# A retrieval-and-projection kernel: loading W in two bursts around tile 0's turn, evacuating before splitting on ScalarE, and giving TensorE two more slots of tile 1

## The reference

```python
retrieved = jnp.mean(item_embeddings[indices], axis=1)         # 512 x 50 indices into a 12500 x 512 table
fused_input = jnp.concatenate([user_rep, retrieved], axis=1)    # 512 x 1024
fused_rep = fused_input @ W_fuse + b_fuse                       # 512 x 512
logits = fused_rep @ W_proj + b_proj                            # 512 x 12500
```

## Time and profile before

| | us |
|---|---|
| median of 3 runs (338.04 to 339.5) | 338.95 |
| the profiled execution | 338.66 |
| its span in the profile | 336.6 |
| TensorE busy (matmuls) | 318.3 (95%) |
| VectorE busy | 184.9 (55%) |
| ScalarE busy | 68.5 (20%) |
| GpSimd busy | 82.3 (24%) |

### The profile page before, as it was taken

The page is one execution under the profiler, slowest core; times in us unless marked ns, Lnnn a source line. Parts: engine busy times, 40 slices in busy tenths (PEclk is TensorE's granted clock), DMA queues, the critical chain, the costliest instruction groups (busy, mean ns, idle before and its releaser), DMA issues.

```text
span 336.6 us, 4239 instructions
## 1 busy us (share of the span) xinstructions
PE 318.3 (95%) x1464; PEld 260.9 (78%) x1464; DVE 184.9 (55%) x317; ACT 68.5 (20%) x102; POOL 82.3 (24%) x84
## 2 busy tenths in 40 slices
PE   4959998599999999999999999999999999999996
PEld 1429876498888898888888888888888888888884
DVE  5899598795678833625454444535354544435222
ACT  2330653530020024022022220222012221020000
POOL 4777778677777100000000000000000000000000
PEclk9996999999999999999999999999999999999999
DMA  7994998989997212786755776568757466442222
GB/s 277 363 396 93 414 383 246 323 270 402 376 338 210 96 62 98 176 333 248 213 162 216 230 243 185 176 249 244 201 161 249 181 213 213 161 166 99 91 91 91
DMA packets 33837, 75.24 MB, mean 224 GB/s; under 512 B 5686, under 2 KB 21830, under 8 KB 33824
## 3 DMA queue, kind: packets, MB, share of 16 engines
q1 hardware_dynamic: 26912, 60.11, 52.2%
q0 software_dynamic: 6336, 13.92, 12.6%
q10 hardware_dynamic: 576, 1.05, 0.8%
HBM read 55.47 MB, written 25.60 MB: 241 GB/s over the span
## 4 chain that ended last, share of the span: by engine, by line
PE 71%; DVE 0%; issue 0%
PE bank L660 69%; PE bank L646 2%; PE bank L636 0%; DVE total L471 0%; DVE out_sb L535 0%
## 5 line engine op out<-in xcount | busy, mean ns | idle before, releaser
L660 PE MATMUL bank<-w_hi,f_hi 128*128 (+1 forms) x400 | 155.8, 390 | 0.0
L660 PE MATMUL bank<-w_lo,f_hi 128*128 (+1 forms) x400 | 155.3, 388 | 0.0
L660 PE MATMUL bank<-w_hi,f_lo 128*128 (+1 forms) x400 | 155.1, 388 | 0.0
L535 DVE TENSOR_TENSOR out_sb<-bank,early 128x500 f32<-128x500 f32 x92 | 62.4, 678 | 128.1 <-PE bank L660 125.5
L660 PEld LDWEIGHTS bank<-w_hi,f_lo 128*128 128x128 f32 x400 | 75.1, 188 | 15.5
L660 PEld LDWEIGHTS bank<-w_hi,f_hi 128*128 128x128 f32 x400 | 75.2, 188 | 15.0
L660 PEld LDWEIGHTS bank<-w_lo,f_hi 128*128 128x128 f32 x400 | 75.2, 188 | 15.0
L327 ACT CAST w_hi<-w_raw 128x1000 fp32r<-128x1000 f32 x46 | 47.1, 1029 | 151.4 <-DMA w_raw<-w_proj 96.4
L267 POOL DMA_INDIRECT ring<-item_embeddings,rows x68 | 71.0, 1045 | 24.8 <-issue 16.6
L507 DVE TENSOR_TENSOR w_lo<-w_raw,w_hi 128x1000 fp32r<-128x1000 f32 (+1 forms) x58 | 55.4, 977 | 2.3 <-ACT w_hi L327 2.3
L471 DVE SCALAR_TENSOR_TENSOR bank<-ring,mask,bank 128x512 f32<-128x512 f32 x56 | 42.1, 752 | 4.5 <-DMA ring<-item_embeddings,rows 1.0
(11 more groups left out here) (60 smaller groups left out, 61.6 us busy)
## 6 DMA issues: line engine op xcount, KB each, us to landing
logits<-out_sb SPq DMA_DIRECT2D x100, 250.0 KB, 2.6
w_raw<-w_proj SPq DMA_DIRECT2D x46, 500.0 KB, 6.9
early<-b_proj SPq DMA_DIRECT2D x25, 250.0 KB, 5.9
early<-w_proj SPq DMA_DIRECT2D x4, 500.0 KB, 6.7
ring<-item_embeddings,rows POOLq DMA_INDIRECT x68, 6.2
early<-user_t ACTq DMA_DIRECT2D x4, 256.0 KB, 4.1
early<-w_fuse SPq DMA_DIRECT2D x4, 256.0 KB, 5.4
wf_ret<-w_fuse SPq DMA_DIRECT2D x1, 1024.0 KB, 19.0
```

What stands on the lines that cost most here:

```text
L535: nc.vector.tensor_tensor(out_sb[:, g % OUT_SLOTS, :], ps[:, 0:CHUNK], bias[:, c % BIAS_SLOTS, 0:CHUNK], ALU.add).then_inc(evacuated, 1)
L660: m = nc.tensor.matmul(ps[:, 0:CHUNK].unsqueeze(1), f[:, t, k, :], w, start=begin, stop=(f is f_lo and k == HK - 1))
```

## The change

Seven edits, all in the order of work:

1. SyncE loads chunks 2 and 3 as soon as slot 12 of tile 0 has landed (before: slot 16), and chunks 4 and 5 when ScalarE has made all of tile 0's `f_hi` (before: right behind chunk 3, where buffers allowed).
2. Chunks 6 and 7 go into the two halves of `early`, no longer into `w_raw`; the eight bias rows are loaded four and four behind the stores of groups 6 and 7, once those halves have been split.
3. ScalarE evacuates groups 0 and 1 before it splits chunks 4 and 5.
4. `PE_LAST` is 4: TensorE sums slots 13 to 16 of tile 1. VectorE's last add for tile 1 is then slot 12, so that the addition of `home` comes last there and writes `total`.
5. The turn of tile t+1 comes behind the whole of group 6, and `fuse` in the middle of group 7.
6. The last eight matmuls of the user half wait one by one for slots 2 to 9 of tile 0.
7. VectorE counts columns (which releases GpSimd's gather of leftovers) behind add 6 of tile 0 (before: add 4), makes `bias_lo` later, and does chunk 1's first low half behind the addition of `home`.

```diff
+BURST_AT = 12
+PACED_AT = 2
-PE_LAST = 2
+PE_LAST = 4
...
         def raw_of(c):
-            return c if c < 4 else c % 2
+            return c % 4 if c < RESIDENT else c % 2
...
             sp.wait_ge(user_fused, 1)
-            sp.wait_ge(slot_landed[place(0, PASSING - 1)], 16 * slot_uses(0, PASSING - 1))
-            for c in range(2, 6):
-                load_chunk(c)
+            sp.wait_ge(slot_landed[place(0, BURST_AT)], 16 * slot_uses(0, BURST_AT))
+            load_chunk(2)
+            load_chunk(3)
+            sp.wait_ge(f_hi_ready, HK)
+            load_chunk(4)
+            load_chunk(5)
             for c in range(RESIDENT):
+                store(0, c)
                 if c < 2:
                     load_chunk(c + 6)
-                store(0, c)
-                if c == RESIDENT - 3:
-                    sp.wait_ge(lo_ready, 8)
-                if c >= RESIDENT - 3:
-                    for b in range(3 * (c - RESIDENT + 3), min(3 * (c - RESIDENT + 4), BIAS_SLOTS)):
+                if c >= RESIDENT - 2:
+                    sp.wait_ge(lo_ready, 2 * c + 2)
+                    for b in range(4 * (c - RESIDENT + 2), 4 * (c - RESIDENT + 3)):
                         load_bias(b)
...
             for c in range(RESIDENT):
-                if c < 2:
-                    split_hi(c + 4)
-                if c == RESIDENT - 2:
+                if c == RESIDENT - 1:
                     mean(1)
-                if c == RESIDENT - 1:
                     fused_hi(1)
                 evacuate_first(c)
                 if c < PE_LAST:
                     keep_last(c)
-                if c in (2, 3):
+                if c < 4:
                     split_hi(c + 4)
...
+                if t and final:
+                    dve.wait_ge(ret_turned, t)
+                nc.vector.tensor_tensor(total[:] if final else total_ps[:], total_ps[:], home[:], ALU.add)\
+                  .then_inc(home_added, 1)
...
-            for i in range(5):
+            for i in range(7):
                 add(0, i)
             count_columns()
-            bias_lo()
-            add(0, 5)
-            add(0, 6)
             split_lo(0, (0,))
             add(0, 7)
             add(0, 8)
+            bias_lo()
...
-            split_lo(1, (0,))
             dve.wait_ge(laps_ready, 1)
             add_home(0)
-            split_lo(1, (1,))
+            split_lo(1)
...
                 for n in range(HK):
+                    if behind is not None:
+                        pe.wait_ge(slot_landed[place(0, behind + n)], 16 * slot_uses(0, behind + n))
...
-                    pe.wait_ge(added, adds_done(1, last_add(1)))
+                    pe.wait_ge(home_added, 2)
...
                     if halfway is not None and k == HK // 2:
-                        turn_sum(halfway)
+                        fuse(halfway)
...
-            user_part(2)
-            user_part(3).then_inc(user_fused, 1)
+            user_part(2, behind=PACED_AT)
+            user_part(3, behind=PACED_AT + HK).then_inc(user_fused, 1)
...
-                    halfway = t + 1 if c == RESIDENT - 2 and t + 1 < TILES else None
-                    project_resident(t, c, halfway)
-                    if halfway is not None:
-                        fuse(halfway)
+                    project_resident(t, c, t + 1 if c == RESIDENT - 1 and t + 1 < TILES else None)
+                    if c == RESIDENT - 2 and t + 1 < TILES:
+                        turn_sum(t + 1)
```

More of the change, by code:

```diff
@@ L153, in raw_of @@
         def raw_of(c):
-            return c if c < 4 else c % 2
+            return c % 4 if c < RESIDENT else c % 2
         def raw_uses(c):
-            return 1 if c < 4 else c // 2
+            return c // 4 + 1 if c < RESIDENT else (c - RESIDENT) // 2 + 3
         def place(t, i):
@@ L192, in load_chunk @@
                     if c >= 4:
-                        sp.wait_ge(lo_ready, 2 * (c - 4 if c < 6 else c - 2) + h + 1)
+                        sp.wait_ge(lo_ready, 2 * (c - 4 if c < RESIDENT + 2 else c - 2) + h + 1)
                     sp.dma_start(raws[raw_of(c)][:, 2 * h:2 * h + 2, :], w_proj[c, :, 2 * h:2 * h + 2, :])\
@@ L455, in count_left, with home_last @@
                 dve.wait_ge(last_landed, 16)
+            def home_last(t):
+                return last_add(t) <= HOME_AFTER
             def add(t, i):
@@ L468, in add @@
                     dve.wait_ge(added, adds_done(t, i - 1))
-                if i == last_add(t):
+                final = i == last_add(t) and not home_last(t)
+                if final:
                     dve.wait_ge(ret_turned, t)
-                nc.vector.scalar_tensor_tensor(total[:] if i == last_add(t) else total_ps[:], here,
+                nc.vector.scalar_tensor_tensor(total[:] if final else total_ps[:], here,
                                                mask[:, t, i + 1:i + 2], total_ps[:], ALU.mult, ALU.add).then_inc(added, 1)
@@ L480, in add_last @@
                     return
-                if t == 1:
-                    dve.wait_ge(home_added, 1)
+                if t == 1 or home_last(t - 1):
+                    dve.wait_ge(home_added, t)
                 else:
@@ L499, in add_home @@
                 dve.wait_ge(home_landed[t], laps * 16)
-                nc.vector.tensor_tensor(total_ps[:] if t else total[:], total_ps[:], home[:], ALU.add).then_inc(home_added, 1)
+                final = t == 0 or home_last(t)
+                if t and final:
+                    dve.wait_ge(ret_turned, t)
+                nc.vector.tensor_tensor(total[:] if final else total_ps[:], total_ps[:], home[:], ALU.add)\
+                  .then_inc(home_added, 1)
             def split_lo(c, halves=(0, 1)):
@@ L608, in _, with user_part @@
         def _(pe):
-            def user_part(k):
+            def user_part(k, behind=None):
                 pe.wait_ge(user_landed[k], 16)
```

## The result

| | before | changed |
|---|---|---|
| median of four runs each, us | 339.23 | 345.61 |
| lowest to highest, us | 338.04 to 339.63 | 344.58 to 347.01 |
| profiled execution, us | 338.66 | 344.58 |
| its span, us | 336.6 | 342.5 |
| mean granted TensorE clock | 0.988 | 0.989 |

The ratio is 1.0197 with a 95% interval of 1.015 to 1.0243: the changed kernel is **slower by about 2%**, where 334.7 us had been forecast in a range of 331.7 to 337.6. The forecast was wrong, and the sign too. Every ratio in this document is taken over those runs of a kernel that lie within 1.5% of its fastest one, which leaves all runs of this pair and of the first batch, but in the later batches only 5 of 25, 12 of 24, 12 of 19 and 12 of 19 runs of the kernel before, and 3 of 10 of x5 in batch 5.

A forecast was written before the change was run, and what follows sets the result against it. TensorE, busy 95% of the span, was taken as the bound. Start -1.9, W -6.1 + 0.3 and slots +1.9 were cut at tile 2's turn to 4.0 us less: 338.66 to 334.7 us, range 331.7 to 337.6.

The forecast's parts named there:

- The start term: Up to tile 0's group 0: pacing, VectorE's order and the early burst together give -1.9 us (-2.3 without contention).
- Rival 2: Start of tile 0: the first burst holds up slot 16, start term +1.1, total 335.3 us; chance 8%.
- W and ScalarE: Tile 0: earlier W and earlier evacuations remove TensorE's stalls, -6.1 us with 0.3 left; ends -6.1 and 0.
- Two more slots: Tile 1's turn: TensorE sums four slots, two more than before, which costs +1.9 us.
- Covered by 1.8 us: Tile 1's turn ends at 62.5, before GpSimd's gathers of tile 2's slots 5 to 8 come up at 64.3.
- Rival 4: Tile 1's turn gates GpSimd's gathers: `home` at 73.9, tile 2 at 103.1, slower at 340.3 us; chance 6%.
- Tile 2's turn: End of tile 1: later place wins 1.36 us, earlier total 2.6; tile 2 starts at 97.4 instead of 101.45.
- the total is ready at 90.4: Tile 2's total, paced by GpSimd's gathers at 1.3 us each, comes 2.6 us earlier than 93.04.
- The three signs of error: Tile 0's last gathers over 5 us, ScalarE getting chunk 7 after 60, GpSimd waiting for TensorE at about 64.

The follow-up runs named there:

- the first batch: Follow-up runs x1 to x4 on the start, beside the kernel before, which took 337.83 us (median of 12 runs).
- x5: x3 with the turns back in the middle of group 6 and fuse between groups 6 and 7; ratios to before 0.9936, 1.0005, 0.9896, 0.9841.
- batch 5: Later follow-up runs of x3, x5 and x12 beside the kernel before, which took 359.63 us there.
- x2: The changed kernel with the column count back behind add 4, burst still at slot 12; 342.92 us, ratio to before 1.0155.
- x3: The changed kernel with the count back behind add 4 and the first burst behind slot 16; 340.69 us, ratio 1.0083; in batch 5 356.6 us, 0.998.
- x1: The changed kernel with the first burst moved back behind slot 16; 343.45 us, ratio to before 1.0181.
- x4: x3 without the pacing of the user half's matmuls; 341.37 us, ratio to before 1.0103.
- x12: x3 with PE_LAST = 2, so two slots fewer on TensorE; 355.01 us, ratio to before 0.9883.
- x6: x3 with chunks 8 and 9 of W loaded later; 353.2, 355.84 and 357.03 us, ratios to before 1.0041, 1.0014, 0.9996.
- x8: The kernel before with chunks 8 and 9 of W loaded later; 358.19 and 357.38 us, ratios to before 1.0073 and 1.0132.

## Why the prediction was wrong, point by point

- **The start term, forecast -1.9, measured +5.4: this is the first step that failed.** Three of its pieces were wrong. Slot 16 was given 1.5 us more by a choice "nearer the first bound" of 2.1 and 6.5 us; slot 13, issued 0.2 us behind the burst, took 7.2, past the far bound. The count of slots behind the burst was wrong: 15 and 16 were named, 13 to 16 it was. Edit 7's later count, which the prediction did not cost, keeps GpSimd waiting 1.83 us and puts slot 13 behind the burst; slot 14 is behind it with the early count too (x2). And the clock, costed as held throughout, fell after the wait (0.66 from 30 to 40 us). Rival 2 named the mechanism but priced it at +1.1 and 8%. With the burst behind slot 16 and the early count (x3) the term is -1.7, where -2.3 had been named without contention: what pacing and VectorE's order bring was put 0.6 us too high.
- The Trainium skill, DMA: Bandwidth & Descriptors (Queues, rings and completion order), which the prediction held against edit 1, says that a DMA engine alternates between its queues packet by packet. Slot 13's 7.2 us against the 2.1 of the earlier trace rows and x2's caught slot 14 agree with it: it should have weighed more than a choice between bounds.
- **W and ScalarE, forecast -6.1 + 0.3: the number came out, under conditions that were not the forecast's.** One stall of 0.65 us is left in tile 0, though chunk 7 came late (ScalarE got its last half at 64.18, where over 60 was named as a sign of error). Chunks 4 to 7 are loaded in step with group 0, so that was 19.7 us behind it, as forecast (57 less 37.2). But from the first burst to group 0 there were 18.3 us, not 10.8. No run had both the early burst and the start at 37: that the stalls would have gone there too is not shown, and x3, with the burst at 31.36, kept 2.2 us of them.
- **Two more slots, +1.9: right** as TensorE's time: 3.57 us from 66.10 to 69.67 for four, against 1.86 for two. **"Covered by 1.8 us" was wrong.** The cover was the distance from the turn's end, put at 62.5, to GpSimd at 64.3. In the changed kernel the gather behind the gate went at 71.5, after 3.4 us of waiting; even in x3, with the good start, it cost 1.5, since the turn of four slots began at 61.53 and ended near 66.1. Rival 4 (6%) had the gate and the place (slot 5), and came true through the late start rather than through a late slot 16 of tile 1. It priced `home` at 73.9 and tile 2 at 103.1; measured were 75.42 and 107.4. The wait for group 5's evacuation, 2.2 us, was no part of the rival.
- **Tile 2's turn, forecast as half a group (1.36 us) won by its place and 2.6 by an earlier total: the second step that failed.** Half a group was booked as won by the later place of the turn. But group 7's bank hangs on group 5's evacuation, which ended at 95.17 before and at 95.03 in x3. The old order asked for it at 98.74, the new one asks at the end of the turn. The prediction asked only what is late next on the way to the total, and not who else TensorE waits for once it is early: 1.9 us in x3, 2.2 in the changed kernel. And "the total is ready at 90.4" took GpSimd's pace for the bound; in x3 it was ready at 92.4. A gather that took 8.1 us to land and the gate stand in its way there; how much each is worth is not shown.
- The three signs of error that were named came true: the last gathers of tile 0 took over 5 us, ScalarE got chunk 7 after 60, and GpSimd waited for TensorE behind 64 us. The clock was 1.0 up to 30 us only, group 0 at 44.5, the burst at 26.27 as forecast, the wait at tile 2's turn 0.73 us at 98.

**What stays open.** x3's one profile has the span of before (336.8 and 336.6), but it is x3's fastest run against the slowest of the kernel before. x3's nine runs go from 338.83 to 342.38, and the median is 2.9 us above before. The three with a mean granted clock of 0.999 or 1.0 took 338.83 to 338.96 us, the six with 0.990 to 0.998 took 340.34 to 342.38. That fits a clock that falls in some runs as it did in tile 1 of x1 and x4, but no slower run of x3 was profiled. How much the turn's place is worth on a chip where before takes 338 us was not measured, and no kernel is shown to beat the one before there. On the other three chips x5's median is 1.5 to 3.9 us lower in four batches, x12's 4.6 and x3's 3.0 in one, x6's 3.2, 0.8 and 0.1; kernels built on the one before idle some 5 us more ahead of tile 0's fuse there, for a reason that was not found, and these gains can't be told apart from that.

## What to carry to other kernels

A bulk load that is started "a little earlier" must be placed by what it is issued ahead of: list the small gathers that still have to go, take their landing time from the worst row in traffic and not from the quiet one, and follow the producer of each gather's operands (here a count moved by two adds) to see at what time it is issued. A step moved forward on the busiest engine spends slack of every operand behind it, buffers that another engine must empty included; ask for each when the other side can deliver, not only for the operand that the move is about. And resources that a moved step frees (four ring slots instead of two) are a gate on whoever fills them, whose cover disappears as soon as anything ahead is late. Last, a wait on the busiest engine can cost twice: once for itself, and once by the clock behind it (1.6 us in x1 and x4).

## What the runs showed of the hardware that was not expected

- One gather issued 0.2 us behind the start of a 2 MB burst on another queue landed in 7.2 us, longer than the three of the earlier trace rows (6.5), against 2.1 in quiet. In x2 one issued 0.4 us behind it landed in 6.5 us, and one issued 1.25 us ahead of it in 3.4 us.
- The clock: 16 recorded matmuls of 128x128 took 2.02 us while TensorE had work in pieces, and 3.75 us after 5.67 us of idle; the windows have 1.00 and 0.66, so the second ran mostly at the lower of the two levels, 1.2 GHz. The Trainium skill, TensorE: Matmul & The Clock Gate (HAM oscillation), says that waits of TensorE for a DMA can bring its clock down; this agrees. x3 and x4 show the stretch with and without pacing, 1.00 against 0.83. Its worth was small, 0.6 us at group 0, where x3's sums wait 0.69 us for slot 13 again.
- One wait of 3.42 us (x1) and one of 2.60 us (x4) in tile 1 went with a lower clock behind them, one of 1.91 (x3) and one of 2.19 (changed) did not.
- The kernel before took 337.83, 356.44, 357.13 and 359.63 us (medians) on four chips. On the slower ones TensorE stands idle with nothing to wait for in the profile; the longest such piece, in x8's second profile, is ahead of tile 0's fuse:

```profile
44.85 5.88 PE L646 MATMUL bank<-ret_t,wf_ret 128*128 128x128 f32 x32 [7.10 <-issue]
```

What it is was not tried.
